# A decoder layer on one core: the prologue's loads and products in another order, and new call sequences on all five engines

## The chip, the cores and the metric

The kernel runs on one core of a Trainium2 chip. The metric is the device time of one execution in microseconds. Below, PE is TensorE, ACT is ScalarE, DVE is VectorE, POOL is GpSimd and SP is SyncE. Each engine works through its own instruction list in order, and waits for the others on semaphores. DMA transfers are issued from SP's, ACT's and POOL's lists. Matmul operands are held as a high and a low part where the kernel wants more digits than one pass gives, and such a product is three matmuls.

## What is computed

The reference, cut to its core. There are four sequences ("rows") of 512 tokens with 512 channels.

```python
def attention(x):            # x normalized, (4, 512, 512)
    xn = layernorm(x, g_norm)
    q, k, v = xn @ Wq, *split(xn @ Wkv)     # 16 heads of 128; one k and v for all
    q, k = l2norm(q * 16) * 4, l2norm(k) * 4
    out = softmax(q @ k.T) @ v              # per head
    return layernorm(out.reshape(..., 2048) @ Wout, g_out)

def ssm(ctx, z):             # state-space branch, 512 channels, 16 states
    xs = conv4(in_proj_w @ ctx);  u = silu(xs + conv_b)
    dt_lo, B, C = split(x_proj_w @ u)
    delta = softplus(dt_proj_w @ dt_lo + dt_proj_b)
    for n in range(16):      # state_t = state_{t-1} * exp(delta * A_n) + delta * u * B_n
        y += C_n * scan(exp(delta * A_n), delta * u * B_n)
    return (y + D * u) * silu(z)

def moe(x):                  # 32 experts of width 192, top 8 of a softmax gate
    return sum(c_e * (silu(x @ Wg_e) * (x @ Wu_e)) @ Wd_e)

x = x + attention(layernorm(x))
x = x + ssm(ctx, layernorm(x))
out = x + moe(layernorm(x))
```

## The kernel before, in words

The kernel has two stages. The first goes through the four rows; the second, behind the last row, works through the experts in blocks of 128 tokens that were sent into lists in HBM by indirect DMA. The change is in the first stage alone.

For each engine the order of work is written out by hand as a sequence of calls of small helpers. There is `first_row()`, run once, `row(b, r)`, run for b = 0, 1, 2 with r = b + 1, and `last_row(b)` for b = 3. A pass of `row(b, r)` holds heads 9 to 15 of row b, its output projection and the beginning of row r up to head 8, so that parts of two rows interleave. What a helper waits for is in the helper; the order of the calls alone sets what is queued behind such a wait.

The helpers that matter here, with the lines of their instructions:

- `norm_tr` (PE, L532) transposes the normalized x, `norm_hi` (ACT, L1258) and `norm_lo` (DVE, L2048) evict it in two parts. `keys_values(r, t)` (PE, L573 to L575) and `q_piece(r, g, t)` (PE, L615 to L617) multiply a tile of 128 tokens with Wkv and with group g of Wq, four heads wide. `squares`, `q_seed` (ACT) and `q_norm` (DVE) find the norms, `q_scaled` (ACT, L1325) evicts, `q_tr` (PE) transposes, `q_copy` (ACT) and `q_lows` (DVE, L2057) evict that.
- For head h: `scores(r, h, k)` (PE, L654 to L658) for four tiles of keys, `exps(r, h, k)` (ACT, L1346), `values(r, h, half)` (PE, L671), `denominators` (DVE, L2130, a reciprocal), `divide` (ACT, L1363), `head_tr` (PE), `head_copy` (ACT, L1372). `out_proj(b, h)` (PE, L694) multiplies head h with its 128 rows of Wout, which `load_wout(b, h)` (SP) brings into one of four slots; it can be issued when the slot's last user, `out_proj(b, h - 4)`, is done.
- The scan: `scan_in(r, e)` (PE, L559) is the input projection, `scan_pad` (ACT) evicts it into x_pad, which is the tile `decay`, `convolution` (DVE, L2033) and `scan_u` (ACT, a silu, L1271) follow, then `scan_params` (PE, L585), `scan_rows` (ACT), `step_size` (PE, L596), `step_parts`, `step_exp`, `step_log` (ACT) and the `softplus` pieces (DVE). For each of the 16 states n: `decays(r, n)` (ACT, L1355, four exponentials, after the scan of n - 1 has read its half of `decay`), `state_input(r, n)` (DVE, L2104), two `state_scan` (DVE, L2112), `state_product` (DVE, L2117), and `add_state(r, n)` (POOL), a DMA that accumulates the product into y. `state_input(r, n)` waits for the accumulate of n - 2 and for the broadcast rows b_bc and c_bc that `load_bc(r, n)` (SP) brings.
- PSUM banks are shared: `bank_q` (the pair) serves norm_tr, scan_in, step_size and q_piece; `bank_s` the scores; `bank_o` the values; `bank_t` keys and values, then head transposes.
- In the prologue Wq (4 MB) is loaded in one DMA into the tile o_t, split into a high and a low part by `split_wq(g)` on ACT and on DVE for each of four groups, and stored to wq_dram by `store_wq(g)`. POOL's `load_wq(r, g)` (L2775) brings a group back into `wq` when the last user of the group before is done. `fill_lists` writes 8.7 MB of blank list entries with one DMA.
- `send_some` (POOL) sends routing entries of the row before. `load_expert` and `split_expert` (ACT) prepare the first experts' weights during row 3.

Engines wait in the prologue as follows: twelve small loads count on one semaphore `w_in_sb`, and PE's first instruction, `neg_rates` on ACT and `conv_start` on DVE wait for all of them. PE's order is scan_in, norm_tr, scan_params, step_size, keys_values, q_piece.

## Time and profile before

| | us |
|---|---|
| median of 3 runs | 1565.39 |
| lowest and highest | 1563.22, 1566.55 |
| the profiled execution | 1556.17 |
| its span | 1554.4 |
| PE busy (matmuls) | 1377.1 |
| DVE busy | 1112.0 |
| ACT busy | 940.6 |
| POOL busy | 479.9 |
| mean granted clock of PE | 0.951 |

Times of the trace are counted from the start of the span. A line of a timeline has the start, the duration, engine, line, operation, destination <- sources, and in brackets the idle time of the engine just before it with what ended it. In views of waits a line reads: the waiting engine and its instruction, what it waited for, then the total in us, the number of times and the longest. Row 0's first scores run at 77 us, its output projection begins at 259, those of rows 1 to 3 at 532, 805 and 1076. The experts begin behind 1172.

### The profile page before, as it was taken

The page shows a single profiled execution, that of the slowest core. Times are in us where ns is not written, and L with a number is a line of the kernel's source. Part 1 is how long each engine was busy: PE and PEld are TensorE (multiplying, and loading weights), DVE is VectorE, ACT ScalarE, POOL GpSimd, SP SyncE. Part 2 cuts the span into 40 slices and gives each one's busy share as a digit, 9 for nine tenths or more (in the row PEclk, how much of TensorE's full clock was granted, in tenths as well). Part 3 has the DMA queues.
Part 4 walks back from the last instruction along what each step waited for, and adds up shares of the span by engine and source line. Part 5 has one row for each costly group of instructions (what it writes and reads, how often), then busy time and mean ns, then how long its engine had stood idle before and what let it go on. Part 6 is the DMA issues. An engine that isn't in the chain of part 4 may idle for free.

```text
span 1554.4 us, 26081 instructions
## 1 busy us (share of the span) xinstructions
PE 1377.1 (89%) x6762; PEld 990.7 (64%) x6763; DVE 1112.0 (72%) x1549; ACT 940.6 (61%) x2422; POOL 479.9 (31%) x367
## 2 busy tenths in 40 slices
PE   4798898999999899999989999999843879999996
PEld 1577676546887554688765468876322667777775
DVE  5365588758889875888987588786885447666663
ACT  3766685457878544787853478786221446666663
POOL 0000010000026340211634021052433776666664
PEclk8899999999999999999999999999975889999998
DMA  6628978621877763187786318766922478898974
GB/s 228 239 91 212 300 207 186 176 70 55 214 206 182 180 168 86 55 207 210 171 188 175 86 55 200 211 136 149 252 64 86 108 174 225 228 235 225 233 183 57
DMA packets 137435, 260.99 MB, mean 168 GB/s; under 512 B 48125, under 2 KB 49614, under 8 KB 128512
## 3 DMA queue, kind: packets, MB, share of 16 engines
q0 software_dynamic: 36480, 122.30, 35.1%
q1 hardware_dynamic: 75120, 86.70, 19.6%
q10 hardware_dynamic: 25744, 50.87, 10.2%
q8 instruction: 45, 0.74, 0.2%
q14 instruction: 46, 0.38, 0.1%
HBM read 170.57 MB, written 46.21 MB: 139 GB/s over the span
## 4 chain that ended last, share of the span: by engine, by line
PE 51%; DMA 20%; DVE 10%; issue 9%; ACT 6%; ACTq 1%; SPq 1%; POOL 1%; POOLq 1%; DVEq 0%
PE bank L694 12%; PE bank L671 9%; DMA out<-y_ring,add_ids 7%; PE bank L654 5%; DMA y<-state 4%; PE pair L615 3%; PE pair L616 3%; PE pair L617 3%; DMA wout<-in_wout 3%; DMA y<-dbu 2%; PE pair L532 2%; PE bank L532 2%; DMA c_bc<-bc_dram 2%; DVE dbu L2112 2%; PE pair L559 1%
## 5 line engine op out<-in xcount | busy, mean ns | idle before, releaser
L694 PE MATMUL bank<-wout,o_t 128*128 128x512 f32 x512 | 240.7, 626 | 26.0 <-DMA wout<-in_wout 16.1
L671 PE MATMUL bank<-v_aug,probs 128*128 128x129 f32 x2048 | 247.9, 277 | 10.4 <-ACT probs L1346 7.2
L671 PEld LDWEIGHTS bank<-v_aug,probs 128*128 128x128 f32 x2048 | 239.3, 192 | 27.4 <-ACT probs L1346 20.2
L2779 POOL DMA_INDIRECT lists<-entry,slot x128 | 196.6, 1536 | 82.9 <-DVE slot L2275 44.2
L694 PEld LDWEIGHTS bank<-wout,o_t 128*128 128x128 f32 x512 | 101.1, 201 | 152.4 <-issue 151.9
L1346 ACT ACTIVATE probs<-bank 128x512 f32<-128x512 f32 x256 | 152.3, 604 | 71.7 <-PE bank L654 32.5
L1355 ACT ACTIVATE decay<-delta,neg_a 128x511 f32<-128x511 f32 x256 | 164.4, 726 | 26.4 <-DVE state L2112 14.4
L2112 DVE TENSOR_TENSOR_SCAN state<-decay,state 128x1024 f32<-128x1024 f32 x64 | 144.7, 2281 | 6.6 <-ACT decay L1355 4.7
L2112 DVE TENSOR_TENSOR_SCAN dbu<-decay,dbu 128x1024 f32<-128x1024 f32 x64 | 144.5, 2279 | 6.5 <-ACT decay L1355 5.6
L2794 POOL DMA_DIRECT2D y<-dbu x32 | 29.1, 910 | 386.0 <-DVE dbu L2117 233.1
L2890 POOL DMA_INDIRECT out<-y_ring,add_ids x68 | 115.0, 1691 | 91.1 <-DMA out<-y_ring,add_ids 64.3
L654 PE MATMUL bank<-q_t,k_t 128*128 128x512 f32 x256 | 127.3, 609 | 1.9 <-ACT q_t L1335 1.9
L2775 POOL DMA_DIRECT2D wq<-wq_dram x30 | 22.0, 768 | 294.0 <-PE pair L617 224.2
L615 PE MATMUL pair<-wq,xn_hi 128*128 128x512 f32 x256 | 109.8, 429 | 2.1 <-ACT q_s L1325 2.1
L1363 ACT ACTIVATE o_s<-bank,den 128x128 f32<-128x128 f32 x256 | 80.0, 373 | 49.0 <-DVE den L2130 43.7
L1160 PE MATMUL bank<-w_hi,xt_hi 128*128 x272 | 99.5, 366 | 10.4 <-DVE xt_lo L2719 10.4
L616 PE MATMUL pair<-wq,xn_hi 128*128 128x512 f32 x256 | 101.6, 397 | 0.0
L617 PE MATMUL pair<-wq,xn_lo 128*128 128x512 f32 x256 | 101.5, 397 | 0.0
L2135 DVE TENSOR_TENSOR w_lo<-w_raw,w_hi (+1 forms) x64 | 95.5, 1492 | 1.9
L2884 POOL DMA_INDIRECT x_blk<-xf_dram,get_ids x70 | 89.7, 1281 | 22.3 <-issue 17.9
L2104 DVE TENSOR_TENSOR state<-du,b_bc 128x2048 f32<-128x2048 f32 x32 | 73.2, 2288 | 29.5 <-DMA y<-state 25.5
L1161 PE MATMUL bank<-w_lo,xt_hi 128*128 x272 | 93.0, 342 | 0.0
(242 smaller groups left out, 2849.4 us busy)
## 6 DMA issues: line engine op xcount, KB each, us to landing
y<-dbu POOLq DMA_DIRECT2D x32, 1024.0 KB, 9.2
wq<-wq_dram POOLq DMA_DIRECT2D x30, 1024.0 KB, 11.4
y<-state POOLq DMA_DIRECT2D x28, 1024.0 KB, 9.8
w_raw<-in_w_exp ACTq DMA_DIRECT2D x32, 768.0 KB
wout<-in_wout SPq DMA_DIRECT2D x64, 256.0 KB, 7.0
b_bc<-bc_dram SPq DMA_DIRECT2D x64, 256.0 KB, 4.1
c_bc<-bc_dram SPq DMA_DIRECT2D x64, 256.0 KB, 5.3
w_raw<-in_w_exp ACTq DMA_DIRECT2D x32, 512.0 KB
```

Source lines behind the costliest of these rows:

```text
L615: pe.matmul(bank_q[t % 2][:], xn_hi[:, k, tile], wq[:, 0, k, :], start=(k == 0), stop=False)
L616: pe.matmul(bank_q[t % 2][:], xn_hi[:, k, tile], wq[:, 1, k, :], start=False, stop=False)
L617: mm = pe.matmul(bank_q[t % 2][:], xn_lo[:, k, tile], wq[:, 0, k, :], start=False, stop=(k == KT - 1))
L654: mm = pe.matmul(bank_s[k % 2][:], k_t[:, tile], q_t[:, j, :], start=True, stop=True)
L671: mm = pe.matmul(bank_o[half][:, (t % 2) * (DH + 1):(t % 2 + 1) * (DH + 1)], probs[:, k, t * P:(t + 1) * P], v_aug[:, k, :], start=(k == 0 ...
L694: mm = pe.matmul((bank_o + bank_s)[t][:], o_t[:, h, t * P:(t + 1) * P], wout[:, h % 4, :], start=(h == 0), stop=(h == H - 1))
L1160: pe.matmul(gu_bank[:, 0:2 * INTER], xt_hi[:, parity, k, :], hi[:, k, :], start=(k == 0), stop=False)
L1346: act.activation(probs[:, k, :], bank_s[k % 2][:], ACT.Exp).then_inc(S["exp_ok"], 1)
L1355: act.activation(dA3[:, e, 1:], delta[:, e, 1:], ACT.Exp, scale=neg_a[:, bass.ds(n, 1), e:e + 1].rearrange("p a c -> p (a c)")).then_inc(S ...
L2112: dve.tensor_tensor_scan(now, dA3[:, es, :].rearrange("p e t -> p (e t)"), now, 0.0, ALU.mult, ALU.add).then_inc(S["scan_ok"], 1)
L2779: pool.indirect_dma_start(out=lists, out_offset=bass.IndirectOffsetOnAxis(ap=slot[:, t, k:k + 1].bitcast(U32), axis=0), in_=entry[:, t, :] ...
L2890: pool.indirect_dma_start(out=out, out_offset=bass.IndirectOffsetOnAxis(ap=add_ids[:, r:r + 1].bitcast(U32), axis=0), in_=y_ring[:, r, :], ...
```

## The change

Prologue:

- The twelve loads on `w_in_sb` are split: `const` and `g_norm` on `const_in`, seven small loads of the scan on `scan_w_in`, three stay. Each user waits for its own group.
- SP issues x, const, g_norm, Wkv, the first quarter of Wq, then the context and w_in, the scan's small loads, the other quarters of Wq, and the rest. Wq is loaded in four quarters with a semaphore each.
- PE's order is norm_tr, keys_values, q_piece(0, 0, 0) and (0, 0, 1), then scan_in, scan_params, step_size, key_tr and the last two query pieces. ACT and DVE follow that order.
- The groups of Wq are split in the order 0, 1, 2, 3. Users wait for the stored group that they need and no longer for all four.
- `fill_lists` is three DMAs of a third each. Part i waits for `oT_ps` of 4 + 2i (that many head transposes) and stands in ACT's order in heads 4, 6 and 8.

All rows: the call sequences of `first_row`, `row` and `last_row` are permuted on every engine, with the same helpers and arguments. Of these the hunks below show the places that the text comes to.

```diff
@@ sp, prologue @@
             load_first(0)
+            sp.dma_start(const[:], a["const"][:, 0:C_ALL]).then_inc(S["const_in"], 16)
+            sp.dma_start(g_norm[:], a["g_norm"]).then_inc(S["const_in"], 16)
+            sp.dma_start(wkv_raw, a["wkv"].rearrange("(k p) n -> p k n", p=P)).then_inc(S["wkv_in"], 16)
+            load_wq(0)
             load_ctx(0)
-            load(const[:], a["const"][:, 0:C_ALL])
-            load(conv_w[:], a["conv_w"].rearrange("(e p) c -> p e c", p=P))
...
+            load_scan(conv_w[:], a["conv_w"].rearrange("(e p) c -> p e c", p=P))
...
+            for g in range(1, G):
+                load_wq(g)
...
@@ sp, row(b, r) @@
                 load_bc(b, 9)
+                next_first(r)
                 load_bc(b, 10)
                 load_bc(b, 11)
-                next_first(r)
+                next_ctx(r)
                 load_bc(b, 12)
                 load_wout(b, 4)
                 load_wout(b, 6)
+                load_wout(b, 5)
                 load_bc(b, 13)
-                next_ctx(r)
-                load_wout(b, 5)
+                load_wout(b, 7)
+                load_wout(b, 9)
+                load_wout(b, 10)
                 load_bc(b, 14)
...
@@ pe @@
-            pe.wait_ge(S["w_in_sb"], 16 * N_W)
+            pe.wait_ge(S["const_in"], 2 * 16)
...
             def scan_in(r, e):
                 pe.wait_ge(S["ctx_in"], r * 32 + 32)
-                if r > 0 and e < 2:
+                if e < 2:
                     pe.wait_ge(S["q_ok"], r * H * 4 + e * 4 + 4)
...
             def first_row():
+                norm_tr(0, 0)
+                norm_tr(0, 1)
+                norm_tr(0, 2)
+                norm_tr(0, 3)
+                keys_values(0, 0)
+                keys_values(0, 1)
+                keys_values(0, 2)
+                keys_values(0, 3)
+                q_piece(0, 0, 0)
+                q_piece(0, 0, 1)
                 scan_in(0, 0)
                 scan_in(0, 1)
                 scan_in(0, 2)
                 scan_in(0, 3)
...
@@ pe, row(b, r) @@
                 out_proj(b, 0)
                 out_proj(b, 1)
+                head_tr(b, 15)
                 out_proj(b, 2)
                 out_proj(b, 3)
-                head_tr(b, 15)
                 norm_tr(r, 0)
+                norm_tr(r, 1)
                 out_proj(b, 4)
                 out_proj(b, 5)
-                norm_tr(r, 1)
                 norm_tr(r, 2)
...
@@ act @@
-            def fill_lists():
-                wq_stored(act)
-                act.dma_start(lists.rearrange("(e p j) c -> p e (j c)", p=P, j=PADS),
...
+            def fill_lists(i):
+                act.wait_ge(S["oT_ps"], 4 + 2 * i)
+                es = slice(i * (NE + 1) // 3, (i + 1) * (NE + 1) // 3)
+                act.dma_start(lists.rearrange("(e p j) c -> p e (j c)", p=P, j=PADS)[:, es],
...
@@ act, row(b, r) @@
+                divide(b, 8, 0)
+                decays(b, 6)
                 exps(b, 9, 0)
                 exps(b, 9, 1)
-                divide(b, 8, 0)
...
                 divide(b, 14, 1)
-                head_copy(b, 14)
+                decays(b, 11)
                 divide(b, 15, 0)
                 divide(b, 15, 1)
                 first_seed(r)
+                head_copy(b, 14)
...
@@ dve, row(b, r) @@
                 state_product(b, 9)
-                state_input(b, 10)
                 denominators(b, 13, 0)
...
                 state_input(b, 11)
+                first_stats(r, 3)
+                denominators(b, 15, 0)
+                first_means(r)
+                denominators(b, 15, 1)
                 state_scan(b, 11, 0)
-                denominators(b, 15, 0)
-                first_stats(r, 1)
-                denominators(b, 15, 1)
...
@@ dve, first_row @@
                 state_scan(0, 3, 1)
-                denominators(0, 5, 1)
+                state_product(0, 3)
                 state_input(0, 4)
...
                 state_scan(0, 4, 1)
-                state_product(0, 3)
...
@@ dve, last_row(b) @@
                 denominators(b, 13, 0)
-                state_input(b, 10)
+                state_product(b, 9)
                 denominators(b, 13, 1)
                 q_lows(b, 3, 3)
+                denominators(b, 14, 0)
                 state_scan(b, 10, 0)
...
                 state_scan(b, 10, 1)
-                denominators(b, 14, 0)
-                denominators(b, 14, 1)
-                state_product(b, 9)
                 state_product(b, 10)
...
@@ pool, row(b, r) @@
                 add_state(r, 1)
                 add_state(r, 2)
-                load_wq(r, 3)
                 add_state(r, 3)
                 add_state(r, 4)
+                load_wq(r, 3)
```

## Rows read from the trace of the kernel before

**Rows 1.** Stretches: length, busy us by engine, granted clock, DMA share, GB/s

```profile
0.00:77.00 77.00, 45.89 (x157) 29.29 (x159) 34.22 (x55) 44.12 (x112) 4.89 (x13) 0.85 0.63 232
77.00:260.00 183.00, 163.63 (x934) 128.62 (x934) 123.12 (x109) 126.99 (x374) 13.54 (x17) 0.97 0.76 204
260.00:532.00 272.00, 260.47 (x1295) 181.96 (x1294) 219.01 (x278) 182.62 (x520) 47.26 (x38) 0.98 0.61 156
1076.00:1172.00 96.00, 67.38 (x188) 34.02 (x188) 74.95 (x78) 27.21 (x46) 35.27 (x25) 0.86 0.66 173
```

**Rows 2.** PE's waits, 0 to 77 us: total, times, longest

```profile
PE pair L559 <- DMA alpha<-in_alpha: 14.2, 1, 14.2
PE pair L532 <- DVE probs L1989: 7.5, 1, 7.5
```

**Rows 3.** Timeline of the prologue (start, us, instruction); one DMA issue with landing time

```profile
6.47 1.29 DVE L1978 BATCH_NORM_STATS2 st<-q_s 128x6 f32<-128x512 f32 x2 [5.48 <-issue]
14.16 9.71 PE L559 MATMUL pair<-q_t,xf 128*128 128x512 f32 x16 [14.16 <-DMA alpha<-in_alpha]
17.12 1.00 DVE L1989 TENSOR_SCALAR probs<-q_s,mv,rs_n 128x512 f32<-128x512 f32 x2
33.24 1.60 DVE L2048 SCALAR_TENSOR_TENSOR xn_lo<-pair,g_norm,xn_hi 128x512 fp32r<-128x512 f32 x2 [1.93 <-ACT xn_hi L1258]
33.26 5.20 PE L585 MATMUL bank<-state,w_x 128*48 128x512 f32 x8
43.24 0.58 PE L573 MATMUL bank<-wkv_hi,xn_hi 128*128 128x256 f32 x1
48.28 0.39 PE L573 MATMUL bank<-wkv_hi,xn_hi 128*128 128x256 f32 x1
51.27 0.40 PE L615 MATMUL pair<-wq,xn_hi 128*128 128x512 f32 x1
...
o_t<-in_wq SPq DMA_DIRECT2D x1, 4096.0 KB, 14.2
```

**Rows 4.** Timelines of DVE, ACT, PE and SP's queue around out_proj of row 1

```profile
528.01 2.29 DVE L2112 TENSOR_TENSOR_SCAN state<-decay,state 128x1024 f32<-128x1024 f32 x1
530.46 1.28 ACT L1363 ACTIVATE o_s<-bank,den 128x128 f32<-128x128 f32 x4 [3.27 <-DVE den L2130]
531.84 15.43 PE L694 MATMUL bank<-wout,o_t 128*128 128x512 f32 x32 [3.50 <-issue]
546.20 1.48 SPq L344 DMA_DIRECT2D wout<-in_wout  x1
554.90 5.37 PE L694 MATMUL bank<-wout,o_t 128*128 128x512 f32 x8 [3.31 <-DMA wout<-in_wout]
604.10 3.60 PE L585 MATMUL bank<-state,w_x 128*48 128x512 f32 x8 [0.40 <-ACT state L1271]
```

**Rows 5.** Row 0: PE's largest wait, the timelines behind it, the fill

```profile
PE bank L656 <- ACT probs L1346: 7.2, 4, 5.1
184.45 2.29 DVE L2104 TENSOR_TENSOR state<-du,b_bc 128x2048 f32<-128x2048 f32 x1 [5.16 <-DMA y<-state]
186.91 0.62 ACT L1363 ACTIVATE o_s<-bank,den 128x128 f32<-128x128 f32 x2 [4.79 <-DVE den L2130]
...
lists<-in_const ACTq DMA_DIRECT2D x1, 8712.0 KB, 61.0
```

**Rows 6.** Row 1 before and at head 9: timelines of POOL, PE, DVE

```profile
439.28 1.46 POOL L2775 DMA_DIRECT2D wq<-wq_dram  x2 [18.64 <-PE pair L617]
459.67 0.88 POOL L2794 DMA_DIRECT2D y<-dbu  x1 [18.02 <-DMA y<-state]
462.39 0.69 PE L615 MATMUL pair<-wq,xn_hi 128*128 128x512 f32 x1
462.72 4.46 DVE L2112 TENSOR_TENSOR_SCAN state<-decay,state 128x1024 f32<-128x1024 f32 x2
```

**Rows 7.** PE's waits, 1076 to 1172 us

```profile
PE bank L694 <- DMA wout<-in_wout: 6.0, 2, 4.7
```

988 lines of the change are left out of this document (498 added, 490 removed).

## The prediction

> **What bounds the kernel now.** I read the busy time by stage first [rows 1]. The profiled execution has a span of 1554.4 us. TensorE (PE) carries 45.9 us of work in the 77 us before the first scores, 163.6 in the 183 us of row 0's heads, and 260.5 in the 272 us from one output projection to the next (the two later stretches of this kind, to 805 and to 1076, look alike: 261 to 262 us busy in 273 and 271). From 1076 to 1172 it is busy 67.4 of 96 us. So the steady rows are bound by PE with some 11 us of idle each, and the change can win only idle time: 31.1 us in the prologue, 19.4 in row 0, about 11 in each of three steady stretches, 28.6 in the last. The expert stage behind 1172 is not touched. The reader should then see whose waits these are [rows 2, 4, 5, 7], and ask in each case whether the new order lets that releaser come earlier.
>
> **The change, part by part.**
>
> *Prologue, loads.* Before, PE, ACT and DVE wait for one semaphore on which twelve small loads count, so PE starts at 14.16 [rows 2]. After, the first PE work is the transposition of the normalized x, which wants x, the constants and g_norm. x is there at 6.47, when its statistics start [rows 3]. The statistics of two tiles take 1.29 us. From 14.2, where the wait ends, to 18.1, where two norms are done, DVE and ACT need 3.9 us for the other two statistics, means, seed, Newton step and two norms; two more norms take 1.0. So the transposes start at 6.5 + 1.3 + 3.9 + 1.0 = 12.7 us. The load order itself gains 1.5 us of PE start, no more.
>
> *Prologue, order of the products.* Two rounds of transpose, eviction high and eviction low took from 31.37, where the 7.5 us of idle ended [rows 2], to 34.84 [rows 3], so 3.5 us; four take 6 to 7: 19. A key and value tile takes 2.9 us at 1.2 GHz (43.24 to 46.10, the next instruction) and 1.5 at 2.4 GHz (two tiles from 48.28 to 51.27) [rows 3]; I take two tiles of each: about 8, to 27. Two query pieces at 2.74 us each (51.27 to 54.01): 32.5. The scan's input projection must then wait for its two banks: squares, seed, Newton step and scaled copies of one piece, about 3 us (an estimate: twelve ACT instructions and two of DVE, and for scale the eviction of two whole tiles by DVE takes 1.6): 35.6. The sixteen matmuls of the input projection take 9.71 after an idle PE [rows 3], to 45.3. In the old order the matmuls of scan_params start at 33.26, which is 9.4 us behind the end of the projection (14.16 + 9.71), with about 2 us of it two transposes that now lie elsewhere: 52.7. They take 5.2, more like 6 when PE was idle before: 58.5. Copy, step sizes and their eight evictions: 7 us (estimate), 65.5, then the last two query pieces, 5.5: 71. Behind them on ACT are key copies, exponential and logarithm over 2048 columns, squares, seed and scaled copies, to about 75.5; two transposes and a copy, and the first scores run at 77.5. Before they run at 77 [rows 1]. **So the prologue is worth nothing, 0.** The new order hides the small loads but hangs the input projection behind the query pieces, and PE is idle for some 7 us between the projection and scan_params where it was idle in that place before as well. Bounds: -4 (the clock is up throughout) to +5 (the copies and table loads on ACT line up badly). The three later quarters of wq, the stores of the split quarters and the loads of b_bc and c_bc lie under this: 4 MB took 14.2 us to land [rows 3], and from about 8 us on that ends near 23, before split_wq(1) to (3) want them.
>
> What the first row shows of the SP queue is that x is used at 6.47 although 1.2 MB were issued behind it within 2 us. The Trainium skill (DMA: Bandwidth & Descriptors, Queues, rings and completion order) says that completion is not first in, first out within an issuing engine. By that rule the first quarter of wq could land with the whole 4 MB at some 23 us instead of at 11, split_wq(0) would hold ACT, which has the key squares behind it, and the prologue would come out up to 5 us longer; by the row, 0. The trace so far speaks for the row.
>
> *Row 0.* PE lost 7.2 us waiting for exponentials [rows 5]. The cause is not ACT: ACT waited 4.8 us for a reciprocal, and DVE was waiting for an accumulate into y with that reciprocal queued behind it. At that time the one 8.7 MB fill of the lists was in flight. The change moves state_product(0, 3) right behind its scan, so that the accumulate starts earlier; puts den(8, 0) behind state_scan(5, 0); issues the fill in three parts, at heads 4, 6 and 8, the last later than the whole was; and computes q_piece(0, 1, *) and the transposes q_tr(0, *, *) some scores earlier. Each part of the fill costs ACT a short wait for a head_tr (under 1 us each, nothing in the trace has it). I take -6, close to the 7.2; bounds -11 (more than half of the 19.4 idle) and +3 (the last part of the fill meets the loads of head 9).
>
> *Three row boundaries.* PE is idle for 3.5 us before out_proj(b, 0) [rows 4]: the divisions of head 15 run only at 530.46, since their reciprocal stood on DVE behind a 2.29 us scan that started at 528.01. In the new order denominators(b, 15, *) stand ahead of state_scan(b, 11, 0), and decays(b, 11) fills ACT while the values of head 15 run. That takes the scan out of the path: -2. Then PE waits 3.31 us for wout [rows 4]. The load for h = 5 was issued at 546.20, behind load_bc(b, 13) and next_ctx(r) in SP's queue. Now wout 4, 6 and 5 go together ahead of both. The load for 5 then waits for out_proj(b, 2), about 10.7 us behind the start of the projection, and needs some 8 us to land (8.6 from 546.20 to the end of PE's wait at 554.90, 8.7), against a need at about 19: nearly the whole 3.3 goes, -2.5. What is late next is scan_params: its silu was on time within 0.4 us, so the scan's tail must move by as much. It can, since norm_tr(r, 1) comes 13 us earlier and DVE no longer waits in norm_lo with scans queued behind it. I take -4 of the 4.5 for each boundary, **-12** in all; bounds -7 and +1 each.
>
> *Steady heads.* 0. Two edits work against the change here. decays(b, 6) now stands ahead of exps(b, 9, 0) on ACT; the scan of n = 5 that it needs ran from 462.72 to 467.18, as head 9 began [rows 6]. The exponentials of head 9, and through bank_s the scores, stand behind it: 0 to +4 us a row, covered by q_piece(b, 3, 0) of 2.74 us. For it, n = 6 can start some 4 us earlier, which supports the boundaries. The second edit is the rival below.
>
> *Last row.* PE waits 6.0 us for wout [rows 7]. The pairs are still loaded in reverse (5 before 4), but state_product(b, 9) comes earlier, so that n = 11 and the load_bc in front of wout 7 to 15 do too, and experts 0 to 2 are loaded during the heads instead of beside the projection. -3, bounds -5 and +3 (these 3.9 MB now beside the accumulates).
>
> **Sum.** 0 - 6 - 12 + 0 - 3 = -21 us on 1554.4, so a span near 1533. The median of the three runs is 1565.39, 11.0 above the span (1556.17 for the profiled execution itself); I keep this distance: **1544 us**.
>
> **Rivals.**
> 1. *The third weight load comes late (slower than before).* load_wq(r, 3) was issued at 439.28, as soon as q_piece(r, 2, 3) was over, and needed at 462.39 [rows 6]: 23 us for 2 MB. It now stands behind add_state(r, 4) on POOL, which was issued only at 459.67, after 18 us of waiting for the previous accumulate. If that time stays, the weights land near 474 and PE stands 11 us in each of three rows: 33 - 21 = +12, 1577. Against it: the 18 us were long because the 2 MB were in flight beside the accumulate, and state_product(r, 3) is now ahead of state_input(r, 4). It decides from the point where add_state(r, 4) is issued later than about 449. Chance 0.15, with smaller forms of it (one row, 1569 and up).
> 2. *The scan's tail is the bound at the boundary.* The 12 us are given back before scan_params, since the scan is paced by accumulates and by c_bc loads and not by DVE's order. Only row 0 and a little of the rest stay, -6: 1559. For it: scan_params was ready just in time. Against it: DVE's waits inside norm_lo. Chance 0.17.
> 3. *Nothing.* PE's work is the same and the idle pieces only change places: 1565. Chance 0.08.
> 4. *More.* The prologue gains its 4 us and the boundaries 7 each: below 1532. Chance 0.05.
>
> **How the numbers follow.** The forecast (1532 to 1556) has 0.55. A measurement of this kernel can tell about 0.2% from no change, 3 us. Faster by more than that: 0.55 + 0.17 + 0.05 = 0.77; within it 0.08; slower 0.15. The range leaves out the 0.05 below and most of rival 1 above: 1531 to 1570.
>
> **What would show it.** Right: first PE work near 12.7; first scores at 77 +/- 4; first out_proj of row 0 near 253, the distance between the first projections of two rows near 268 instead of 272; PE's wait before out_proj(b, 0) near 1.5 and no wait for wout above 1; scan_params without a new wait. Wrong: a PE wait for wq in q_piece(r, 3, 0); a PE wait for silu before scan_params that was 0.4; exps(b, 9, 0) behind decays by more than 3 us; accumulates into y of 15 us or more between 150 and 230; first scores later than 82.

## The result, and the profile after

The changed kernel takes 1517.33 us (median of 4 runs, 1510.96 to 1518.72) against 1564.61 for the kernel before (4 runs, 1563.22 to 1566.55): ratio 0.970, 95% interval 0.965 to 0.975. It is 47 us faster where 21 were forecast, and below the range that was given. The profiled execution has a span of 1516.7 us, 37.7 less than the span of before.

First the stretches, to be held against [rows 1]. Columns: length, busy us and instructions by engine, granted clock of TensorE, DMA share, GB/s.

```profile
0.00:83.00 83.00, 49.39 (x163) 30.95 (x165) 33.77 (x54) 44.67 (x112) 4.89 (x13) 0.84 0.60 209
83.00:250.00 167.00, 157.12 (x928) 124.28 (x927) 122.68 (x114) 125.87 (x375) 14.12 (x17) 1.00 0.85 226
250.00:513.00 263.00, 257.88 (x1295) 181.48 (x1295) 218.75 (x278) 182.07 (x521) 35.03 (x32) 0.99 0.64 162
1044.00:1140.00 96.00, 70.10 (x196) 37.83 (x196) 76.09 (x87) 29.66 (x49) 28.03 (x17) 0.82 0.52 131
```

The first numbers behind the length are PE. Row 0 lost 16 us of length and only 6.5 of busy time; the steady row lost 9, of which 6.4 are idle time (11.5 to 5.1) and 2.6 busy time, with the same 1295 matmuls and a granted clock of 0.99 instead of 0.98.

All stages are compared by four marks read off the timelines of PE and ACT: the first exponential of row 0 (end of the prologue), the first projection matmul of row 0, that of row 3, and the end. The four stages and the span are those of one profiled execution of each kernel. "Timed" is the median of all runs; these are 2 for o_DVE, n_ACT_PE, k2 and p1 and 4 to 10 for the others. Each group of kernels was timed beside the kernel before on its own chip, where that kernel's median lay between 1558.0 and 1569.9 us, so compare the ratios and not the medians.

| kernel | prologue | row 0 | rows 1 to 3 | rest | span | timed, us | ratio to before |
|---|---|---|---|---|---|---|---|
| before | 78.8 | 180.6 | 816.4 | 478.5 | 1554.4 | 1564.6 | |
| after | 83.2 | 166.6 | 794.5 | 472.4 | 1516.7 | 1517.3 | 0.970 |
| h1_new_first | 82.8 | 171.3 | 816.3 | 486.2 | 1556.6 | 1563.6 | 0.998 |
| h2_new_rows | 81.6 | 177.3 | 791.2 | 480.9 | 1530.9 | 1534.9 | 0.981 |
| f1_one_fill | 83.2 | 176.2 | 794.8 | 479.1 | 1533.2 | 1535.2 | 0.978 |
| f2_before_3fills | 78.6 | 173.4 | 817.4 | 491.0 | 1560.4 | 1560.6 | 0.989 |
| g1_wout | 75.7 | 178.8 | 810.5 | 486.6 | 1551.5 | 1566.8 | 1.000 |
| g2_den15 | 81.0 | 176.7 | 822.8 | 486.2 | 1566.7 | 1566.2 | 1.000 |
| g3_both | 77.9 | 176.3 | 812.5 | 487.7 | 1554.5 | 1558.6 | 0.997 |
| g4_dec6 | 82.0 | 167.1 | 797.9 | 480.4 | 1527.4 | 1527.1 | 0.974 |
| o_SP | 83.4 | 181.2 | 837.2 | 479.1 | 1580.9 | 1586.2 | 1.014 |
| o_DVE | 82.8 | 182.8 | 913.4 | 479.3 | 1658.3 | 1661.4 | 1.057 |
| o_POOL | 82.4 | 168.8 | 830.2 | 477.9 | 1559.3 | 1562.8 | 0.995 |
| n_ACT_PE | 75.2 | 192.3 | 904.5 | 489.7 | 1661.7 | 1668.0 | 1.062 |
| k1_pool_dec6 | 83.6 | 172.6 | 829.4 | 470.9 | 1556.4 | 1555.1 | 0.998 |
| k2_pool_input5 | 81.7 | 168.8 | 809.2 | 468.6 | 1528.3 | 1535.2 | 0.984 |
| p1_sp_den | 78.9 | 182.8 | 833.7 | 476.7 | 1572.1 | 1573.4 | 1.010 |
| m1_old_start | 75.4 | 173.9 | 794.1 | 470.4 | 1513.7 | 1519.1 | 0.977 |
| m2_early_loads | 68.9 | 172.7 | 792.4 | 474.7 | 1508.6 | 1510.2 | 0.969 |
| m3_best | 70.3 | 165.8 | 800.5 | 475.6 | 1512.2 | 1504.8 | 0.965 |

Of the 37.7 us, the prologue gave back 4.4, row 0 won 14.0, rows 1 to 3 won 22.0 (9.4, 10.5 and 2.0) and the rest 6.1.

How far one execution can be trusted is in the table too. The same old prologue ends at 75.2 to 81.6 us in nine kernels (mean 78.1), the new one at 81.7 to 83.6 in nine (mean 82.8). The "rest" holds the expert stage, which no edit touches: from the first matmul on an expert block to the end it takes 342.9 to 346.4 us in seven of the kernels and 349.1 to 353.6 in the other thirteen. The kernels before and after are both among the seven; where one of the seven is set against one of the thirteen, 3 to 10 us of the difference come from there.

The boundary of row 1 after, against [rows 4]. Columns of a timeline: start, us from the first start of the group to its last end, engine, line, operation, out<-in, count, idle time ahead and its releaser.

```profile
511.77 0.17 DVE L2147 RECIPROCAL den<-bank 128x2 f32<-128x2 f32 x1 [0.45 <-PE bank L669]
511.87 2.29 DVE L2129 TENSOR_TENSOR_SCAN state<-decay,state 128x1024 f32<-128x1024 f32 x1
512.76 7.10 PE L692 MATMUL bank<-wout,o_t 128*128 128x512 f32 x16 [1.10 <-issue]
516.47 8.93 SPq L349 DMA_DIRECT2D wout<-in_wout  x3
520.14 7.03 PE L692 MATMUL bank<-wout,o_t 128*128 128x512 f32 x16
535.19 3.60 PE L692 MATMUL bank<-wout,o_t 128*128 128x512 f32 x8
578.82 3.60 PE L587 MATMUL bank<-state,w_x 128*48 128x512 f32 x8 [0.66 <-ACT state L1275]
```

The reciprocal now stands ahead of the scan, PE waits 1.10 us instead of 3.50, and no wait for wout is left. Sixteen projection matmuls take 7.1 us and eight take 3.6. In [rows 4] the first 32 took 15.43, 1.5 more than the 13.97 that the same 32 take in row 0, and the eight behind the wait for wout 5.37, 1.8 more. The granted clock behind the two waits in the kernel before (stretches as above, PE alone), then the 32 of row 0:

```profile
532.00:536.00 4.00, 4.00 (x7) 0.65 0.06 10
552.00:556.00 4.00, 1.10 (x2) 0.91 0.82 237
556.00:560.00 4.00, 4.00 (x7) 0.66 1.05 243
560.00:564.00 4.00, 4.00 (x17) 1.00 0.80 236
...
259.43 13.97 PE L694 MATMUL bank<-wout,o_t 128*128 128x512 f32 x32 [2.28 <-issue]
```

So in row 1 each of the two waits was paid for twice, once as idle time and once as matmuls behind it that ran in part at 1.2 GHz. The two waits and what followed them make 2.40 + 1.46 + 3.31 + 1.77 = 8.9 us; from the first exponential of row 1 to that of row 2 the kernel won 10.4. This second price isn't paid every time: behind the 2.28 us of row 0, in the line above, the 32 matmuls ran at full speed.

Row 3 won only 2.0 us. The stretch from the projection of row 2 to the first exponential of row 3 won 4.9 like the one before it, but the heads of row 3 take 171.1 us instead of 168.3. The kernel after has a new wait there, for a head's scaled values, and value products behind it at a granted clock of 0.50 to 0.89 (1024 to 1028 us); the first line shows 32 of them undisturbed.

```profile
935.08 3.74 PE L669 MATMUL bank<-v_aug,probs 128*128 128x129 f32 x32
1021.96 0.66 PE L536 MATMUL bank<-const,o_s 128*128 128x128 f32 x4 [2.18 <-ACT o_s L1367]
1022.45 5.47 PE L669 MATMUL bank<-v_aug,probs 128*128 128x129 f32 x32
```

### The profile page after: what moved, and what is told of

Read it like the earlier page. It is cut to its first block, busy times and chain, and to the rows that moved or that the text cites. A ratio compares the mean times of both kernels' runs of the same rounds, so it can differ in the third digit from the quotient of the medians.

```text
span 1516.7 us, 26103 instructions
## 1 busy us (share of the span) xinstructions
PE 1369.6 (90%) x6762; PEld 990.2 (65%) x6763; DVE 1109.6 (73%) x1549; ACT 939.3 (62%) x2422; POOL 485.4 (32%) x367
## 4 chain that ended last, share of the span: by engine, by line
PE 52%; DMA 19%; issue 11%; DVE 9%; ACT 5%; POOL 2%; POOLq 1%; SPq 1%; ACTq 0%; DVEq 0%
DMA out<-y_ring,add_ids 14%; PE bank L669 12%; PE bank L692 10%; PE bank L652 6%; PE pair L613 3%; PE pair L615 3%; PE pair L614 3%; PE bank L536 3%; DMA y<-state 2%; PE pair L536 2%; PE bank L654 2%; DVE dbu L2046 1%; PE bank L656 1%; PE bank L655 1%; PE pair L596 1%
## 5 line engine op out<-in xcount | busy, mean ns | idle before, releaser
L2804 POOL DMA_INDIRECT lists<-entry,slot x128 | 199.8, 1561 | 134.3 <-DVE slot L2299 96.6
L692 PE MATMUL bank<-wout,o_t 128*128 128x512 f32 x512 | 231.2, 606 | 4.3 <-issue 4.3
L1359 ACT ACTIVATE decay<-delta,neg_a 128x511 f32<-128x511 f32 x256 | 165.1, 719 | 50.3 <-DVE dbu L2129 31.4
L692 PEld LDWEIGHTS bank<-wout,o_t 128*128 128x128 f32 x512 | 97.8, 195 | 123.5 <-issue 123.2
L2913 POOL DMA_INDIRECT out<-y_ring,add_ids x68 | 122.0, 1795 | 86.5 <-DMA out<-y_ring,add_ids 58.8
L1914 ACT ACTIVATE y_ring<-bank,meta 128x512 f32 x68 | 46.8, 688 | 74.4 <-PE bank L1179 74.4
L1162 PE MATMUL bank<-w_hi,xt_lo 128*128 x272 | 92.4, 340 | 0.0
## 6 DMA issues: line engine op xcount, KB each, us to landing
y<-state POOLq DMA_DIRECT2D x28, 1024.0 KB, 10.5
```

The source lines that it names most:

```text
L692: mm = pe.matmul((bank_o + bank_s)[t][:], o_t[:, h, t * P:(t + 1) * P], wout[:, h % 4, :], start=(h == 0), stop=(h == H - 1))
L1359: act.activation(dA3[:, e, 1:], delta[:, e, 1:], ACT.Exp, scale=neg_a[:, bass.ds(n, 1), e:e + 1].rearrange("p a c -> p (a c)")).then_inc(S ...
L2804: pool.indirect_dma_start(out=lists, out_offset=bass.IndirectOffsetOnAxis(ap=slot[:, t, k:k + 1].bitcast(U32), axis=0), in_=entry[:, t, :] ...
L2913: pool.indirect_dma_start(out=out, out_offset=bass.IndirectOffsetOnAxis(ap=add_ids[:, r:r + 1].bitcast(U32), axis=0), in_=y_ring[:, r, :], ...
```

## The experiments

**Which part holds which gain.** Two kernels between the two.

```diff
h1: kernel after
-    row, last_row on PE, ACT, DVE, POOL, SP: order of after
+    row, last_row on PE, ACT, DVE, POOL, SP: order of before
h2: kernel before
-    row, last_row on the five engines: order of before
+    row, last_row on the five engines: order of after
```

> The changed kernel's prologue and first row (up to head 8, with the list fill in three parts) with the old order of calls in all rows behind. Leaves nothing out. Theory (the gain of row 0 comes from the fill and the first row's own order, the rest from the rows' order): the prologue is 4 us longer than in the kernel before, row 0's heads 9 to 15 keep nearly all of the 16 us that they won, the later rows win nothing: about 1552 us. Rival (heads 9 to 15 won their 16 us by the rows' new order on DVE, ACT and PE): nothing is left but the longer prologue, 1567 to 1570 us.

> The kernel before with its own prologue, first row and single fill, but with the changed kernel's order of calls in the rows and in the last row on all five engines. Leaves nothing out. Theory (fill): row 0's heads 9 to 15 stay at the old 78 us, boundaries and steady heads win their 25 to 28 us: about 1531 us. Rival (order of the rows): heads 9 to 15 win their 16 us too and the old prologue keeps its 4 to 6: 1511 to 1515 us.

h1: 1563.6 us, ratio 0.998 (0.994 to 1.002); row 0 won 9.3, rows 1 to 3 nothing. That lies between the theory and its rival. h2: 1534.9 us, 0.981 (0.974 to 0.989); row 0 won 3.3 and rows 1 to 3 all of their gain, 25.3. The sum is near the theory's, but its account of row 0 is not right: heads 9 to 15 win with the old fill too (66.3 us instead of 78.5), and what they win is lost before head 9 (111.0 instead of 102.1). Neither cause was right for row 0 alone.

**The fill of the lists.**

```diff
f1: kernel after
-    fill_lists(0), (1), (2) at heads 4, 6, 8
+    fill_lists() whole, behind head_copy(0, 3)
f2: kernel before
-    fill_lists() whole, behind head_copy(0, 3)
+    fill_lists(0) behind q_copy(0, 1, 3); (1) behind exps(0, 6, 2); (2) behind q_copy(0, 2, 2)
```

> The changed kernel with the fill of the lists as one transfer of 8.7 MB again, issued behind head_copy(0, 3) as in the kernel before. Theory (fill): the accumulates that meet it are late again, row 0's heads 9 to 15 lose 10 to 16 us: 1528 to 1533 us. Rival (order): within 3 us of the changed kernel, 1514 to 1520 us.

> The kernel before with only the fill changed: three transfers of 2.9 MB at heads 4, 6 and 8 instead of one. Theory (fill): row 0 wins 10 to 16 us, 1549 to 1555 us. Rival (order): within 3 us of the kernel before, 1562 to 1568 us.

f1: 1535.2 us, 0.978 (0.972 to 0.985); row 0 is 9.5 us longer than after. f2: 1560.6 us, 0.989 (0.980 to 0.997); row 0 7.2 shorter than before. Both are less than the 10 to 16 that the theory gave. The DMA view of row 0, after and then f1 (KB of one, median us to landing), PE's wait for exponentials in f1, and what DVE waited for ahead of it:

```profile
lists<-in_const ACTq DMA_DIRECT2D x3, 2904.0 KB, 13.2
...
lists<-in_const ACTq DMA_DIRECT2D x1, 8712.0 KB, 59.9
PE bank L652 <- ACT probs L1350: 8.7, 2, 6.9
186.91 2.29 DVE L2118 TENSOR_TENSOR state<-du,b_bc 128x2048 f32<-128x2048 f32 x1 [12.63 <-DMA c_bc<-bc_dram]
```

In the kernel after this wait is 1.9 us. One transfer of 8.7 MB was in flight for 60 us beside the accumulates and loads; three take 13 each (21 in f2) with pauses between. In the kernel before it was an accumulate that held DVE, with the reciprocal behind it [rows 5]; in f1 it is the load of c_bc, for 12.6 us, and most of f1's loss lies before head 9 (112.0 us from the first exponential instead of 104.1), where the theory had it in heads 9 to 15 (64.2 instead of 62.5). So that the single fill is what costs the time is shown, that the accumulates alone carry it is not. The fill is worth 7 to 10 us of row 0, the rest is the first row's order together with the rows': h1 has the split fill and the new first row and wins 9.3, with the rows' order it is 14.0.

**The two waits that the forecast named.** One line on SP, two on DVE, both.

```diff
g1, g3: kernel before, SP, row
     load_wout(b, 6)
+    load_wout(b, 5)
     load_bc(b, 13)
     next_ctx(r)
-    load_wout(b, 5)
g2, g3: kernel before, DVE, row
     state_input(b, 11)
+    denominators(b, 15, 0)
+    denominators(b, 15, 1)
     state_scan(b, 11, 0)
-    denominators(b, 15, 0)
     first_stats(r, 1)
-    denominators(b, 15, 1)
```

> The kernel before with one line moved on SP: in the rows 0 to 2 load_wout(b, 5) stands ahead of load_bc(b, 13) and next_ctx(r). Theory (a wait of 3.3 us in front of a projection matmul also lowers TensorE's clock for the five matmuls behind it, which took 1.06 us each instead of 0.59): the stretch from the first projection matmul to the first exponential of the next row loses the 3.3 and some 1.9 us more, 5 us in each of three rows: about 1550 us against 1565. Rival (the wait alone): 3.3 or less in each row, 1555 to 1558 us, and the same number of slow matmuls elsewhere.

> The kernel before with two lines moved on DVE: in the rows 0 to 2 denominators(b, 15, 0) and (b, 15, 1) stand ahead of state_scan(b, 11, 0). Theory: the wait of 3.5 us before out_proj(b, 0) becomes about 1.1, and the four matmuls behind it that took 1.06 to 1.19 us come back to 0.6: 4.4 us in each row that had the 3.5 us wait, 2 us or more in row 0: about 1554 us. Rival (the wait only changes its cause, or the scan's tail is late by as much at scan_params): 0 to 2 us a row, 1559 to 1565 us.

> The kernel before with both of these moves, three lines in all. Theory: they add up, 9.4 us in each of three rows: about 1537 us, and the new order of all other calls in the rows is worth next to nothing. Rival (the other edits on PE, ACT, DVE and POOL carry the gain, or what is late next takes it back at scan_params): 1548 us or more.

g1: 1566.8 us, 1.000 (0.997 to 1.003); g2: 1566.2, 1.000 (0.997 to 1.004); g3: 1558.6, 0.997 (0.994 to 1.001). The kernel before took 1566.7 us beside them. All three theories missed their totals, and g1's rival did too; g2's comes near, g3's holds. In the place itself the theory of g1 holds: from the first projection matmul of row 1 g1 comes to the next exponentials in 97.7 us, where the kernel after takes 97.7 and before took 102.5. But in row 0 the wait for wout moved to a later load, 30.8 us behind the first projection matmul instead of 21.5, and g2 and g3 opened new waits. PE in g2, then in g3, then in g1 in row 0:

```profile
546.76 0.66 PE L532 MATMUL pair<-const,probs 128*128 128x128 f32 x4 [1.41 <-DVE probs L1989]
553.94 6.67 PE L694 MATMUL bank<-wout,o_t 128*128 128x512 f32 x8 [3.08 <-DMA wout<-in_wout]
...
543.06 0.66 PE L532 MATMUL pair<-const,probs 128*128 128x128 f32 x4 [1.48 <-DVE probs L1989]
556.32 3.67 PE L694 MATMUL bank<-wout,o_t 128*128 128x512 f32 x8 [0.99 <-DMA wout<-in_wout]
...
285.24 5.07 PE L694 MATMUL bank<-wout,o_t 128*128 128x512 f32 x8 [2.92 <-DMA wout<-in_wout]
```

The norms of the next row now stood behind the waiting reciprocals, 1.4 us late for PE. And eight projection matmuls behind a wait show what it costs in clock: 3.67 us behind 0.99 of idle, 5.07 behind 2.92, 5.37 behind 3.31, 6.67 behind 1.41 and 3.08. But the length of the wait alone doesn't set that price. The kernel before in row 2, then n_ACT_PE (below) in row 1, waits of 2.8 and 3.3 us that cost no clock, with a granted 1.00 on both sides:

```profile
829.20 3.67 PE L694 MATMUL bank<-wout,o_t 128*128 128x512 f32 x8 [2.76 <-DMA wout<-in_wout]
...
596.61 3.67 PE L694 MATMUL bank<-wout,o_t 128*128 128x512 f32 x8 [3.30 <-DMA wout<-in_wout]
```

What decides between the two was not settled. So the two fixes alone are worth 4.0 of 22.0 us in rows 1 to 3; the gain needs the orders around them.

**SP's whole order with these denominators.**

```diff
p1: kernel before
-    SP, row: order of before
+    SP, row: order of after
     DVE, row: denominators(b, 15, *) ahead of state_scan(b, 11, 0), as in g2
```

> The kernel before with SP's new order of calls in the rows 0 to 2 and the two denominators(b, 15, *) ahead of state_scan(b, 11, 0); PE, ACT and POOL as before. The three lines moved by themselves won only 4 us between the first and the last projection because the 2 MB of the context were then issued 14 us into the projection, ahead of wout 7 to 10, and PE waited 1 to 4 us for those. Theory (the rest of SP's order takes these loads out of the way): the stretches from the first projection matmul to the next row's first exponential go from 104, 101 and 100 to about 98 to 99 us each, the heads stay at 168.5: 806 us from the first to the last projection instead of 812 and 816, and some 1545 to 1550 in all. Rival (SP's new order only fits the new order of DVE and PE): 812 or more.

1573.4 us, 1.010 (1.002 to 1.018), two timed runs: 1% slower than before. The theory falls; the stretch behind out_proj is 99.2 us in row 0, but 104.4 in the next two, and heads 9 to 15 take 78 to 81 us instead of 70 to 78. DVE, ACT and PE late in row 1, then SP's wait and two of its issues:

```profile
521.61 2.29 DVE L2104 TENSOR_TENSOR dbu<-du,b_bc 128x2048 f32<-128x2048 f32 x1 [11.25 <-DMA c_bc<-bc_dram]
524.08 0.62 ACT L1363 ACTIVATE o_s<-bank,den 128x128 f32<-128x128 f32 x2 [8.65 <-DVE den L2130]
524.67 0.77 PE L656 MATMUL bank<-q_hi,k_hi 128*128 128x512 f32 x1 [9.50 <-issue]
...
SPq L316 <- PE pair L532: 19.1, 1, 19.1
508.73 0.38 SPq L316 DMA_DIRECT2D q_s<-in_x  x1
509.71 1.57 SPq L357 DMA_DIRECT2D c_bc<-bc_dram  x1
```

c_bc lands 11 us late, a reciprocal is queued behind the waiting input on DVE, and PE stands for 9.5. The load of n = 10 is now queued on SP behind next_first(r), and SP stood for 19.1 us in front of it, for the last transpose of queries (L532), which PE's old order has later than its new one. The load was issued at 509.71; in the kernel before the one of n = 10 was issued at 501.51. The rival, that SP's new order only fits the new order of the others, holds.

**One engine's order put back, or two put in.**

```diff
o_SP, o_DVE, o_POOL: kernel after
-    row on this engine: order of after
+    row on this engine: order of before
n_ACT_PE: kernel before
-    row on PE and ACT: order of before
+    row on PE and ACT: order of after
```

> The changed kernel with SP's order of calls in the rows 0 to 2 as before (the loads of wout, b_bc, c_bc, context; the last row and the first stay new). Theory (the load order carries the boundary): PE waits about 3.3 us for wout in the middle of the projection again and runs at 1.2 GHz for some 4 us behind it, so the stretch from the first projection matmul to the first exponential goes from 97.6 back to about 102.5 us, the heads keep their 165: 15 us in all, about 1532. Rival (the orders of PE, ACT and DVE leave the load enough room): less than 2 us a row, 1517 to 1523.

> The changed kernel with DVE's order of calls in the rows 0 to 2 as before. Theory: the reciprocal of head 15 is behind the scan of n = 11 again and PE waits 3.5 us before out_proj(b, 0) with slow matmuls behind it, and norm_tr(b + 1, 1), now early on PE, waits for norms that DVE makes late: 4.5 us or more in each of three rows from the first and up to as much from the second, 1531 to 1545. Rival (the wait only moves): within 5 us of the changed kernel, 1513 to 1523.

> The changed kernel with POOL's order of calls in the rows 0 to 2 as before: load_wq(r, 3) ahead of add_state(r, 3) again, load_wq(r, 0) behind add_state(b, 7), the sends spread otherwise. Theory (the forecast's first rival named this queue; the trace of the changed kernel shows no wait for the weights): no difference above 2 us, 1514 to 1520. Rival (two fewer megabytes beside the accumulates 3 and 4 are what let the steady heads win): 3 us or more in each of three rows, 1526 or more.

> The kernel before with the changed kernel's order of calls on PE and ACT in the rows 0 to 2, DVE, POOL and SP as before. Theory (heads 9 to 15 win by PE and ACT, about 3 us a row beside the wait at out_proj): the heads go from 170.5 to 167 or less while the wait before out_proj(b, 0) and the wait for wout stay, and norm_tr(r, 1) waits for its norm: 1555 to 1562 us. Rival (PE's and ACT's order is worth nothing without DVE's): heads stay at 170, boundaries at 102 or more, 1565 or more.

o_SP 1586.2 us, 1.014 (1.009 to 1.019); o_DVE 1661.4, 1.057 (1.050 to 1.065); o_POOL 1562.8, 0.995 (0.991 to 0.999); n_ACT_PE 1668.0, 1.062 (1.052 to 1.071). o_DVE and n_ACT_PE have two timed runs each. Every theory was missed, all on the same side, and only the open-ended rivals of o_POOL and n_ACT_PE held, the latter without its reason: the heads did not stay at 170 us. An order taken out of its set costs more than the set is worth. In o_SP PE waits for wout for 8.8, 7.3 and 4.0 us in the three projections, where the theory took 3.3, and for scaled values for 17.4 us in all. In o_DVE and n_ACT_PE, which share the old DVE with the new PE and ACT, DVE's reciprocals wait 79 and 77 us for value products in two rows, PE's largest waits are the same to 0.1 us (16.5 for scaled queries, 9.5 for exponentials, 8.4 for DVE's norms), and the heads of rows 1 and 2 take 205.6 and 205.0 us in o_DVE, 201.5 and 201.6 in n_ACT_PE, instead of 165.0 and 165.1.

**The path of POOL's order.** In o_POOL, where only sends, loads of wq and accumulates are in another order, the trace shows four engines in a chain:

```profile
424.78 1.46 POOL L2800 DMA_DIRECT2D wq<-wq_dram  x2 [15.77 <-PE pair L615]
426.24 0.93 POOL L2819 DMA_DIRECT2D y<-state  x1
441.15 2.29 DVE L2121 TENSOR_TENSOR state<-du,b_bc 128x2048 f32<-128x2048 f32 x1 [10.31 <-DMA y<-state]
443.62 0.63 ACT L1367 ACTIVATE o_s<-bank,den 128x128 f32<-128x128 f32 x2 [5.86 <-DVE den L2147]
444.30 1.11 PE L536 MATMUL bank<-const,o_s 128*128 128x128 f32 x4 [4.92 <-ACT o_s L1367]
```

and the kernel after in the same place:

```profile
417.27 0.87 POOL L2819 DMA_DIRECT2D y<-state  x1 [11.02 <-DMA y<-dbu]
428.25 2.29 DVE L2121 TENSOR_TENSOR state<-du,b_bc 128x2048 f32<-128x2048 f32 x1
429.23 1.53 POOL L2800 DMA_DIRECT2D wq<-wq_dram  x2
```

load_wq(r, 3) waits for PE's last use of the old weights, and the accumulate of n = 3 is queued behind it: it is issued 75.7 us behind the row's first exponential, in the kernel after 69.5. state_input(r, 5) waits for this accumulate, the reciprocals of heads 6 and 7 stand behind it on DVE, behind these the scaling on ACT, then PE. Two candidates for the place where this reaches PE, each with POOL's old order:

```diff
k1: ACT
-    decays(b, 6)
     exps(b, 9, 0)
     exps(b, 9, 1)
+    decays(b, 6)
k2: DVE
-    state_input(r, 5)
     denominators(r, 6, 1)
     ...
     q_lows(r, 2, 3)
+    state_input(r, 5)
```

> The changed kernel with two edits: POOL's old order of calls in the rows 0 to 2, and decays(b, 6) back behind exps(b, 9, 1) on ACT in all rows. POOL's old order alone cost 14 us a row, all of it before the exponentials of head 9. Theory (the loss reaches PE through one place: load_wq(r, 3) holds up the accumulates 3 and 4, the scan of n = 5 is 11 us late, and decays(b, 6) in front of the exponentials of head 9 waits for it): with the decays behind, the stretch from the first exponential to head 9's goes from 111 back to about 101 to 103 us and the whole to 1525 to 1535. Rival (the late accumulates hold PE in other places too, or the scan's tail carries the delay to the projection): 1545 us or more.

> The changed kernel with two edits: POOL's old order of calls in the rows 0 to 2 (which alone cost 14 us a row) and state_input(r, 5) on DVE back behind q_lows(r, 2, 3), where it stood before. In the trace with POOL's old order, state_input(r, 5) waits 10.3 us for the accumulate of n = 3, the reciprocals of head 7 are queued behind it, ACT waits 5.9 us for them and PE 4.9 for the scaled values. Theory (that is the path): the exponentials of heads 7 to 9 come back, the stretch from the first exponential to head 9's goes from 111 to 101 to 104 us, and the whole to 1530 to 1540. Rival (the scan of n = 5 itself, later still, holds decays(b, 6) and with it the exponentials of head 9): still 109 us or more, 1550 or more.

k1: 1555.1 us, 0.998 (0.995 to 1.001), rows 1 to 3 829.4 us against 830.2: the decays are not the place; the rival holds. k2: 1535.2 us (two runs), 0.984 (0.979 to 0.989), a total as the theory had it; the stretch to head 9 of row 1 is 105.0 us against 111.4, 1 us above the theory's, and 809.2 for the three rows: state_input(r, 5) carries 21 of the 36 us that POOL's old order costs. The other 15 are 2.4 us before head 9, 3.4 in heads 9 to 15 (65.7 instead of 62.3) and 1.2 from the projection to the next exponential in each of rows 1 and 2. Of the 3.4, PE's wait before the first projection matmul makes 2.7 (3.81 us instead of 1.10), and the sixteen matmuls behind it take 10.0 instead of 7.1. Why this wait is longer wasn't traced.

**The decays alone.**

```diff
g4: kernel after, ACT, row and last_row
-    decays(b, 6)
     exps(b, 9, 0)
     exps(b, 9, 1)
+    decays(b, 6)
```

> The changed kernel with decays(b, 6) back behind exps(b, 9, 1) on ACT in all rows. Theory (the exponentials of head 9 wait behind it for the scan of n = 5): the stretch from the first exponential of a row to that of head 9, 102.7 us in rows 1 to 3 against 100.8 before, comes back to about 101, and heads 9 to 15 keep their 62.3: 2 us a row and 3 or more in row 0, some 8 us in all, 1509 us. Rival (the scan of n = 6 comes later and the scan's tail gives it back at scan_params or in the products of the last row): 1515 to 1519 us.

1527.1 us, 0.974 (0.968 to 0.980), no gain, and more than the rival allowed: PE was idle 2.4 us in the heads of row 1 with either order. The 2 us by which head 9 starts later after the change are work that PE does ahead of it. Of the 10.7 us by which the profiled span is longer than that of the kernel after, 8.0 lie in the rest. In rows 1 and 2 g4's heads are 3 us longer, and only by the clock; in row 3 they are 2.9 shorter. PE at one place of row 1, g4 first, then after:

```profile
426.00:430.00 4.00, 4.00 (x24) 0.68 0.58 135
430.00:434.00 4.00, 4.00 (x21) 0.50 0.95 130
...
426.00:430.00 4.00, 4.00 (x35) 1.00 0.49 114
430.00:434.00 4.00, 4.00 (x27) 1.00 0.95 184
```

**The prologue, and a version that keeps the better of both.**

```diff
m1: kernel before
+    row, last_row of after on the five engines; fill in three parts as in f2
m2: m1
+    const, g_norm on one semaphore, the seven scan weights on another; w_gate, g_out, alpha behind wq
-    DVE: conv_start between the statistics, first_norm(0, 2), (0, 3) behind the convolution
+    DVE: all statistics and norms, conv_start, convolution(0, 0), norm_lo(0, 0), (0, 1), convolution(0, 1)
+    ACT: norm_hi(0, *) ahead of scan_u(0)
+    PE: scan_in(0, *), norm_tr(0, *), scan_params(0)
m3: m2
+    PE, ACT, DVE from the first scores on, and SP's loads of b_bc and c_bc: first row of after
```

> A kernel between the two: prologue and first row (to head 8) of the kernel before, but with the list fill in three parts, and all rows in the changed kernel's order. Theory (the parts add up where they meet in order: the old prologue is 2 to 4 us shorter, the fill in three parts gives row 0 its 9 us, the rows their 25): some 1507 to 1515 us, 2 to 8 below the changed kernel. Rival (the first row's new order is needed for the rows' new order in heads 9 to 15): 1520 us or more.

> The same kernel between the two, with one thing more: the small loads in groups as in the changed kernel (each engine waits only for its own), the products still in the old order, input projection first, and all four norms and transpositions ahead of the convolution's second half and of scan_params. Theory (the old order of the products with early loads takes out both idle stretches, the wait of 14.2 us before the first matmul and the 7.5 us before the transpositions): first exponentials at 70 to 74 us instead of 79 and 83, and 1500 to 1508 us. Rival (the chain input projection, convolution, silu, scan_params sets the end of the prologue, and it starts no earlier than the context lands): 77 us or more, no gain on the kernel without it.

> The kernel between the two with early small loads and the old order of the products in the prologue (first exponentials at 68.9 us), and now also the changed kernel's order of calls from the first scores on in row 0. Theory: row 0 takes the changed kernel's 104 + 62.5 us instead of 108.3 + 64.4, all else stays: 1502 to 1508 us, 3.5 to 4.2% below the kernel before on the same chip. Rival (row 0's first heads are paced by the stores and loads of the query weights, which now lie elsewhere): no gain, 1508 to 1512.

m1 1519.1 us, 0.977 (0.971 to 0.984), between the theory and the rival and no better than the kernel after; m2 1510.2, 0.969 (0.964 to 0.975), with the prologue that the theory had or a little better and a total 2 us above it; m3 1504.8, 0.965 (0.962 to 0.968), as the theory had it. PE's waits in the prologue, after and then m2:

```profile
PE pair L536 <- DVE probs L2000: 12.4, 1, 12.4
PE bank L587 <- ACT state L1275: 8.6, 1, 8.6
PE pair L561 <- ACT q_s L1329: 3.6, 1, 3.6
...
PE pair L562 <- DMA xf<-in_w_in_t: 9.9, 1, 9.9
PE bank L590 <- ACT state L1280: 4.9, 1, 4.9
```

The grouped loads are good, the new order of products is not: with the input projection first, and the loads grouped, the prologue ends at 68.9 us instead of 83.2. (m2 also moves norms and transposes, so not all of this is the order of the products.) And the new first row, put behind it (m3), takes 165.8 instead of 172.7. In m3's profiled execution rows 1 to 3 take 800.5 us, 8.1 more than in m2; it was the slowest of its six, 1514.0 us, where four took 1504.2 to 1505.2. m3's ratio to before lies below that of the kernel after; the two were not timed side by side, and the intervals overlap (0.962 to 0.968, 0.965 to 0.975), so that it also beats the kernel after is likely, not shown.

## Why the prediction was wrong, step by step

**Prologue: 0 forecast, +4.4 measured.** PE started at 12.41 (forecast 12.7), the input projection at 35.78 (35.6), scan_params at 53.20 (52.7). The step that failed is the last one, "then the last two query pieces, 5.5: 71": they ran from 65.9 to 73.9, 8.0 us, the first of them at 1.2 GHz (its twelve matmuls took 5.1). This is not what was left of PE's 8.6 us wait before scan_params, since the clock had come back in between. It fell again from 64 us on, behind the step sizes, with waits of only 0.68, 0.59 and 0.40 us among them (PE alone, as above):

```profile
59.00:62.00 3.00, 2.01 (x5) 1.00 1.03 420
62.00:65.00 3.00, 2.93 (x7) 0.81 0.93 365
65.00:69.00 4.00, 3.60 (x11) 0.50 0.02 5
```

The kernel before had shown such a price: its last two query pieces took 8.1 us, from 62.2 to 70.2, and the forecast took 2.74 each from the two that ran at full clock. Behind them PE waits 4.6 us for scaled queries, as before, and does one more q_tr before the first scores at 81.2. The bound of +5 held. The rule on completion order (the Trainium skill, DMA: Bandwidth & Descriptors, Queues, rings and completion order) did not price this kernel: ACT splits the first quarter of wq at 17.92 right behind the norms, with no wait.

**Row 0: -6 forecast, -14.0 measured.** The step that failed is "I take -6, close to the 7.2". The mechanism was the right one in the main and the term too small: only PE's wait for exponentials was taken. f1 and f2 price the fill at 7 to 10 us, since several smaller waits and the clock behind them go too (granted 0.97 to 1.00). The rest is the new order; 1.2 us of it is the wait before the first projection, 2.28 to 1.09. The measured -14.0 is beyond the bound of -11.

**Boundaries and steady heads: -12 and 0 forecast, -22.0 measured.** Both waits went as forecast (1.1 us left before out_proj, none for wout), and what came next, scan_params, waits 0.66 us. The step that failed is "I take -4 of the 4.5": it counts idle time alone, and less of it than went. At the three boundaries 15.6 us of the two kinds of wait went (4.4, 5.7 and 5.5), where 12 were taken. Behind the old waits lay 8.1 us of slow matmuls (1.8, 3.2 and 3.1; the last are 32 in 17.04 us instead of 13.97), for which the sum has no term. For row 1 they can be read in [rows 4] itself, as 15.43 us for 32 matmuls and 5.37 for 8. The Trainium skill (TensorE: Matmul & The Clock Gate, HAM oscillation — how this bites in real kernels) says that a wait for data between groups of matmuls lets the clock fall back to half. [rows 4] agrees, and so do the waits of 2.92 us in g1, 1.41 and 3.08 in g2 and 2.18 in row 3 of the kernel after; those of 2.28 and 2.76 us in the kernel before and of 3.30 in n_ACT_PE, with matmuls at full speed behind them, do not. The steady heads, taken at 0, won 5.5 and 5.6 us in rows 1 and 2, of which 4.4 are the wait before out_proj, and lost 2.8 in row 3 by the new wait shown above.

**Last row: -3 forecast, -3.9 measured, and 2.2 more in the stage behind.** The 6.0 us for wout [rows 7] went to 0, but PE's next wait, for DVE, grew from 16.5 to 17.6. From the first projection matmul of row 3 to PE's first matmul of the expert stage, before and then after:

```profile
1194.99 2.72 PE L1145 MATMUL bank<-const,cols_f 128*1 128x128 f32 x12 [7.65 <-DVE cols_f L2708]
...
1159.44 2.72 PE L1145 MATMUL bank<-const,cols_f 128*1 128x128 f32 x12 [7.66 <-DVE cols_f L2730]
```

That is 119.1 and 115.2 us. The other 2.2 of the 6.1 in the table are differences of the expert stage, where nothing was changed.

**Spans against timed runs: 0 forecast, -9.6 measured.** The step that failed is "I keep this distance": I added the 11 us between the span of the profiled execution and the median to the new span. For the changed kernel the distance is 0.6. What differs between executions is the granted clock. Of the 25 runs of the kernel before that stood beside g1 to g4, spans go from 1555.5 to 1582.5 us at mean clocks of 0.950 to 0.936, 13 us for a hundredth; in the other four groups of 11 or 13 runs it is 9 to 19. The profiled execution had 0.951, as high as the highest of all 75 such runs, so it was a lucky one to set out from; the kernel after runs at 0.952 to 0.956. In the profiled executions much of the spread is the start of the expert stage, which no edit touches. PE behind row 3's projection, after and then f2:

```profile
1174.30:1274.30 100.00, 87.31 (x426) 0.92 0.69 170
...
1199.40:1299.40 100.00, 72.06 (x340) 0.83 0.56 133
```

Why the changed kernel is granted more clock in its timed runs too was not settled: fewer waits are an argument, no experiment isolates it.

**The rivals.** The first, that load_wq(r, 3) comes late behind add_state(r, 4), was false. PE never waited for the weights in q_piece(r, 3, 0), and add_state(1, 4) was issued at 428.69. The rival looks at what the load would wait for and not at what waited behind it: in [rows 6] the load had stood for 18.64 us for PE, with accumulate 3 in the queue behind it. Moving it back is what the new DVE order lives on, 12 us a row by o_POOL. The second, the scan's tail as the bound, is out: scan_params waits 0.66 us where it waited 0.40. The third is out as well. The fourth, "more", had a chance of 0.05 and named the side on which the result fell; its boundaries of 7 each were near (6.2, 8.9 and 8.6 with the slow matmuls), its prologue was not, and the rest of the miss it doesn't have.

## What to carry to other kernels

An order of calls on one engine is tuned to those on the others: changes that are worth 22 us as a set were worth 4 by the three moves that look like the cause, and 36 to 119 us of loss when one engine's part was taken out. Price the set by the waits that end in it, and don't expect its parts to add up. Count a wait in front of matmuls together with the matmuls behind it, whose duration in the same row tells the clock; do it for each wait by itself, since its length doesn't tell whether the clock fell. A median to come is not the new span plus the old distance: look at the clock of the profiled execution against those of the timed ones first. And before a difference of a few us is given to an edit, look at how much a stage that wasn't edited differs.

## What the runs showed of the hardware

The granted clock can fall with no idle time ahead. In g4 it went to 0.50 at 428 to 434 us, behind 16 value products (2.0 us in all) and 32 router products (4.1 us), back to back; in the kernel after the same instructions ran at 1.00 within a microsecond of the same place. It happened in rows 1 and 2 of g4 and not in row 3, and cost 3 us a time. What decides it stays open.

A wait can leave the clock up or bring it down at one and the same length. In front of projection matmuls, waits of 2.76, 3.21 and 3.30 us (before, and n_ACT_PE twice) were followed by eight matmuls in 3.67 us, waits of 3.21 and 3.31 in the kernel before by eight in 5.37. In g1 a wait of 2.54 us before the projection cost nothing in row 1, where 32 matmuls took 13.97 us, and a wait of 2.18 us in row 3 of the kernel after cost 1.7.
